# A gated cross-attention and mixture-of-experts block: Wout summed on VectorE, the last rounds reordered on each engine, the first list and rows fetched ahead of the stage barrier

## What is computed

```
x = x + tanh(g_xattn) * xattn(layernorm(x), ctx, ctx, mask)     # ctx: 8 x 722 x 512
x = x + tanh(g_ffn)   * moe(layernorm(x))

xattn: q = query@Wq+bq; k = key@Wk+bk; v = key@Wv+bv            # 32 wide
       s = q k^T / sqrt(512); s = (s - mean(s)) / (std(s) + eps)
       head = softmax(s + mask_term) @ v
       return tile(head, 16) @ Wout + bout                      # Wout: 512 x 512
moe:   p = softmax(x@router_w.T); w, idx = top_k(p, 2); w = w / (sum(w) + 1e-6)
       y = (silu(x@w13[:, :I]) * (x@w13[:, I:])) @ w2            # I = 1024, per expert
       return sum of w * y over the token's 2 experts
```

## Time and profile before

| | us |
|---|---|
| median of 3 runs | 453.95 |
| lowest and highest | 451.54, 454.06 |
| profiled execution, its own time | 455.68 |
| span of the profiled execution | 454.1 |
| stage one up to the barrier, in that span | 130.3 |
| start of the first product of tile 0 | 143.0 |
| start of the last tile's products | 425.0 |

### The profile page before, as it was taken

One profiled execution on the slowest core, in us unless ns is written; L12 is line 12 of the kernel. 1 busy time (PEld: TensorE's weight loads), 2 busy tenths in 40 slices (PEclk: granted clock), 3 DMA queues, 4 the chain that ended last, 5 costly groups with the idle time before them and its releaser, 6 DMA issues.

```text
span 454.1 us, 7292 instructions
## 1 busy us (share of the span) xinstructions
PE 391.5 (86%) x2056; PEld 288.7 (64%) x2057; DVE 232.1 (51%) x512; ACT 193.9 (43%) x314; POOL 123.0 (27%) x214
## 2 busy tenths in 40 slices
PE   2979989995105999999989999999999999999990
PEld 2425655553003878778767787787877878778780
DVE  2215665756681239528795223852962674565120
ACT  1123543432750247428765224643842662573220
POOL 2311354443412130412232123041122204314301
PEclk9989986976555999999999999999999999999997
DMA  8955779811106919727797221971774577201011
GB/s 260 370 192 180 270 230 367 313 50 37 36 0 206 396 25 282 274 64 214 255 387 296 84 46 27 279 289 33 228 258 145 129 287 225 46 0 29 19 27 15
DMA packets 17554, 78.01 MB, mean 172 GB/s; under 512 B 3618, under 2 KB 4770, under 8 KB 10372
## 3 DMA queue, kind: packets, MB, share of 16 engines
q1 hardware_dynamic: 11060, 66.79, 41.2%
q0 software_dynamic: 4720, 7.78, 8.9%
q10 hardware_dynamic: 1760, 3.28, 2.2%
HBM read 71.20 MB, written 7.54 MB: 173 GB/s over the span
## 4 chain that ended last, share of the span: by engine, by line
PE 75%; DVE 9%; issue 5%; ACT 3%; POOL 2%; DMA 2%; DVEq 1%; ACTq 1%; POOLq 0%
PE turnA L438 20%; PE scp L458 20%; PE turnB L438 18%; PE kvp L307 4%; PE kvp L445 3%; PE turnA L325 2%; PE scp L425 2%; DVE w13l L785 2%; PE scp L331 1%; PE turnA L363 1%; DMA xg<-xn_d,gidx 1%; DVE x L749 1%; ACT kv L504 1%; DVE bns L698 1%; PE turnA L356 1%
## 5 line engine op out<-in xcount | busy, mean ns | idle before, releaser
L785 DVE TENSOR_TENSOR w13l<-stage,w13h 128x1024 fp32r<-128x1024 f32 x64 | 76.4, 1219 | 3.8 <-ACT w13h L561 3.3
L561 ACT ACTIVATE w13h<-stage 128x1024 fp32r<-128x1024 f32 x64 | 64.5, 1052 | 0.1
L438 PE MATMUL turnA<-w13h,xTh 128*128 128x512 f32 x128 | 53.2, 415 | 5.0 <-DVE xTl L868 5.0
L458 PE MATMUL scp<-w2h,hTh 128*128 128x512 f32 x128 | 55.7, 435 | 1.2 <-DVE hTl L879 1.2
L438 PE MATMUL turnB<-w13h,xTh 128*128 128x512 f32 x128 | 51.9, 405 | 0.0
L438 PE MATMUL turnA<-w13h,xTl 128*128 128x512 f32 x128 | 51.3, 401 | 0.0
L438 PE MATMUL turnA<-w13l,xTh 128*128 128x512 f32 x128 | 51.3, 401 | 0.0
L458 PE MATMUL scp<-w2l,hTh 128*128 128x512 f32 x128 | 50.6, 395 | 0.0
L438 PE MATMUL turnB<-w13h,xTl 128*128 128x512 f32 x128 | 50.5, 395 | 0.0
L438 PE MATMUL turnB<-w13l,xTh 128*128 128x512 f32 x128 | 50.5, 394 | 0.0
L458 PE MATMUL scp<-w2h,hTl 128*128 128x512 f32 x128 | 50.2, 392 | 0.0
(11 more groups left out here) (162 smaller groups left out, 649.6 us busy)
## 6 DMA issues: line engine op xcount, KB each, us to landing
stage<-in_w_dram SPq DMA_DIRECT2D x48, 1024.0 KB, 6.9
ctx_t<-in_ctx_dram SPq DMA_DIRECT2D x8, 1444.0 KB, 9.0
x_t<-in_x_dram SPq DMA_DIRECT2D x8, 200.0 KB
xT_t<-in_xT_dram SPq DMA_DIRECT2D x8, 200.0 KB, 10.6
out_dram<-x ACTq DMA_DIRECT2D x8, 200.0 KB
xn_d<-xn ACTq DMA_DIRECT2D x8, 200.0 KB
stage<-in_wout_dram SPq DMA_DIRECT2D x1, 1024.0 KB, 11.8
ent_next<-lists_d POOLq DMA_DIRECT2D x17, 1.0 KB, 2.0
```

Source lines behind the costliest of these rows:

```text
L438: mm = pe.matmul(region, xp[:, c, :], wp[:, q, c, :], start=(c == 0 and i == 0), stop=(c == HC - 1 and i == 2))
L458: mm = pe.matmul(scp[:, 512:512 + H], hp[:, q, j * P:(j + 1) * P], wp[:, q * QC + j, :], start=(q == 0 and j == 0 and i == 0), stop=(q == ...
L561: act.activation(dst, src, ACT.Copy).then_inc(S["w_hi"], 1)
L785: dve.tensor_tensor(lo, raw, hi.bitcast(F32), ALU.subtract).then_inc(S["w_lo"], 1)
```

## The change

1. The sum of `Wout`'s four row blocks of 128 moves to VectorE: three adds of 128x512 (`add_wout`) between `make_values(0)` and `ln1_stats(2)`. TensorE then needs one product with `sel` per strip, where it had four, and adds `bout` with a product of one row, `ident[0:1, 0:D]`, so that `bout` is loaded once, to one row. `wraw` and its zeroing are gone; ScalarE scales with `g_t` while it copies to `wsum`, and VectorE's step between is gone. `sum_weights` stands ahead of `turn_query(1)`.
2. The transposes of `wsum` and the products with the router weights move to round 1: `turn_weights` behind `project(1)`, `route_weights` behind `scores(1)`, with the wait for `wx9` ahead of `heads(0)`. The transposes go to `outp`, so `turn_values(1)` waits for `wsumT_copied`. VectorE's copy to `wx9` stands behind `score_stats(1)`.
3. SyncE loads `bout`, then batch 1's context, then `Wout`, where it had `Wout`, `bout` twice, then the context.
4. TensorE's wait for `zero_made` moves from ahead of all rounds to `turn_values(0)`; `headT` is no longer zeroed.
5. VectorE: `finish_sigma(i)` stands ahead of `make_weights(i-2)` and `raw_logits(i-1)` in every round. After round 8 it runs `choose(7)`, `make_weights(6)`, `add_attention(7)`, `make_places(7)`, the tile tables, `make_weights(7)`, then its count on `attn_done`, and only then the splits of expert 0's units 0 to 7.
6. ScalarE: in round 8 `copy_head(7)` follows `copy_probT(7)`, ahead of the transfer and the normalisation of batch 6. Its splits 0 to 7 stand behind its count on `attn_done`.
7. GpSimd: `scatter` no longer waits for the scatter before it; in round 9 `scatter(6)` stands ahead of `norm2(7)`. The list entries and rows of tile 0 are fetched (`fetch_first`) before its count on `attn_done`; `xg`, `ent_next` and `gidx` get SBUF of their own for it.
8. `heads(b)` waits for `lg_made`, `outputs(b)` for `x2_ready` of the batch before.

```diff
@@ SyncE
+            sp.dma_start(bout_r[:], bout.rearrange("(o d) -> o d", o=1)).then_inc(S["bout_in"], 16)
+            load_ctx(1)
             sp.dma_start(stage2[:, 0:HC, :], Wout.rearrange("(c p) n -> p c n", p=P)).then_inc(S["wout_in"], 16)
-            sp.wait_ge(S["wraw_zero"], 1)
-            for r in range(2):
-                sp.dma_start(wraw[VW * r + D:VW * r + D + 1, :], bout.rearrange("(o d) -> o d", o=1)).then_inc(S["bout_in"], 16)
-            load_ctx(1)
@@ TensorE
             def turn_values(b):
                 pe.wait_ge(S["kv_copied"], b + 1)
+                if b == 0:
+                    pe.wait_ge(S["zero_made"], 1)
+                if b == 1:
+                    pe.wait_ge(S["wsumT_copied"], 1)
@@ heads, outputs
+                if b >= 1:
+                    pe.wait_ge(S["lg_made"], b)
...
+                if b >= 1:
+                    pe.wait_ge(S["x2_ready"], b)
...
             def sum_weights():
-                pe.wait_ge(S["wout_in"], 16)
+                pe.wait_ge(S["wout_added"], 3)
+                pe.wait_ge(S["bout_in"], 16)
                 pe.wait_ge(S["v_made"], 1)
-                for c in range(HC):
-                    for r in range(2):
-                        mm = pe.matmul(outp[r * VW:r * VW + D, :], sel[:], stage2[:, c, :], start=(c == 0), stop=(c == HC - 1))
+                for r in range(2):
+                    pe.matmul(outp[r * VW:r * VW + D, :], sel[:], stage2[:, HC, :], start=True, stop=True)
+                    mm = pe.matmul(outp[r * VW + D:(r + 1) * VW, :], ident[0:1, 0:D], bout_r[:], start=True, stop=True)
                 mm.then_inc(S["wsum_done"], 1)
+
+            def turn_weights():
...
+            def route_weights():
                 pe.wait_ge(S["wsumT_copied"], 1)
-                pe.wait_ge(S["q_fixed"], 4)
+                pe.wait_ge(S["q_fixed"], 6)
@@ TensorE, rounds
                 if live(i):
                     project(i)
+                if i == 1:
+                    turn_weights()
...
                     scores(i)
+                if i == 0:
+                    sum_weights()
+                if i == 1:
+                    route_weights()
+                    pe.wait_ge(S["wx9_made"], 1)
                 if live(i - 1):
                     heads(i - 1)
                 if live(i + 1):
                     turn_query(i + 1)
-                if i == 0:
-                    sum_weights()
@@ ScalarE, rounds
+                if i == NB:
+                    copy_head(i - 1)
                 if live(i - 2):
+                    if i >= NB:
+                        store_x2(i - 2)
                     normalise2(i - 2)
                     logit_exp(i - 2)
-                if live(i - 1):
+                if live(i - 1) and i < NB:
                     copy_head(i - 1)
...
-                if i == NB + 1:
-                    for unit in range(0, 2 * NQ):
-                        split_hi(0, unit, None)
             act.drain().then_inc(S["attn_done"], 1)
+            for unit in range(0, 2 * NQ):
+                split_hi(0, unit, None)
@@ VectorE, rounds
+                if i == NB + 1:
+                    break
...
                 if live(i - 2):
                     make_places(i - 2)
+                if live(i):
+                    finish_sigma(i)
+                if live(i - 2) and i < NB:
                     make_weights(i - 2)
                 if live(i - 1):
                     raw_logits(i - 1)
-                if live(i):
-                    finish_sigma(i)
-                if i == NB + 1:
-                    for unit in range(0, 2):
-                        split_lo(0, unit)
+            choose(NB - 1)
+            make_weights(NB - 2)
+            add_attention(NB - 1)
+            make_places(NB - 1)
...
-            for unit in range(2, 2 * NQ):
+            make_weights(NB - 1)
+            dve.drain().then_inc(S["attn_done"], 1)
+            for unit in range(0, 2 * NQ):
                 split_lo(0, unit)
-            dve.drain().then_inc(S["attn_done"], 1)
@@ GpSimd
                 for k in range(2):
-                    if b >= 1:
-                        pool.wait_ge(S[f"lists_put{k}"], 16 * b)
...
-                if live(i - 2):
+                if live(i - 2) and i <= NB:
                     norm2(i - 2)
                 if live(i - 3):
                     scatter(i - 3)
+                if i == NB + 1:
+                    norm2(i - 2)
...
+            def fetch_first():
+                pool.dma_start(ent_next[:], lists_d[0:P, :]).then_inc(S["list_in"], 16)
+                for k in range(2):
+                    pool.wait_ge(S[f"xn2_put{k}"], 16 * NB // 2)
+                gather(0)
...
+            fetch_first()
+            for k in range(2):
+                pool.wait_ge(S[f"out_put{k}"], 16 * NB // 2)
+            pool.drain().then_inc(S["attn_done"], 1)
+            pool.wait_ge(S["attn_done"], 4)
             pool.wait_ge(S["tiles_ready"], 1)
-            fetch(0)
             entries_stay(0)
```

More of the change, by code:

```diff
@@ L87, in gated_block @@
         tile_row = sb(es, "tile_row", [1, TILES], I32)
+        xg = sb(es, "xg", [P, H])
+        ent_next = sb(es, "ent_next", [P, 2], I32)
+        gidx = sb(es, "gidx", [P, 1], I32)
         a = ExitStack()
@@ L110, in gated_block @@
         wqr = sb(a, "wqr", [P, HC, VW + E])
-        wraw = sb(a, "wraw", [P, H])
+        bout_r = sb(a, "bout_r", [1, H])
         wsum = sb(a, "wsum", [P, H])
@@ L383, in _ @@
             pe.wait_ge(S["sel_made"], 1)
-            pe.wait_ge(S["zero_made"], 1)
             pe.wait_ge(S["wqr_made"], 3)
@@ L539, in copy_qT, with scale_weights, copy_turned_weights, store_x2 @@
                 act.activation(qT[b % 2][:], qTp, ACT.Copy, scale=float(H) ** -0.5).then_inc(S["qT_copied"], 1)
-            def wsum_steps():
+            def scale_weights():
                 act.wait_ge(S["wsum_done"], 1)
-                act.wait_ge(S["wraw_zero"], 1)
-                for r in range(2):
-                    act.activation(wraw[r * VW:r * VW + D, :], outp[r * VW:r * VW + D, :], ACT.Copy).then_inc(S["wraw_set"], 1)
+                act.wait_ge(S["tanh_done"], 1)
+                act.activation(wsum[:], outp, ACT.Copy, scale=g_t[:, 0:1]).then_inc(S["wsum_made"], 1)
+            def copy_turned_weights():
                 act.wait_ge(S["wsum_turned"], 1)
-                act.activation(wsumT[:].rearrange("p c s -> p (c s)"), turnB[:, 0:HC * P], ACT.Copy).then_inc(S["wsumT_copied"], 1)
+                act.activation(wsumT[:].rearrange("p c s -> p (c s)"), outp, ACT.Copy).then_inc(S["wsumT_copied"], 1)
+            def store_x2(b):
+                act.wait_ge(S["x2_ready"], b + 1)
+                act.dma_start(out[b], x2[b % 2][:]).then_inc(S[f"out_put{b % 2}"], 16)
             def split_hi(e, unit, last):
@@ L685, in make_values @@
                     dve.wait_ge(S["emask_made"], 1)
-                    dve.wait_ge(S["zero_made"], 1)
                 if b >= 2:
@@ L785, in split_lo, with add_wout, copy_low_weights @@
                 dve.tensor_tensor(lo, raw, hi.bitcast(F32), ALU.subtract).then_inc(S["w_lo"], 1)
-            def wsum_steps():
-                dve.wait_ge(S["wraw_set"], 2)
-                dve.wait_ge(S["bout_in"], 32)
-                dve.wait_ge(S["tanh_done"], 1)
-                dve.tensor_scalar(wsum[:], wraw[:], g_t[:, 0:1], None, ALU.mult).then_inc(S["wsum_made"], 1)
+            def add_wout():
+                dve.wait_ge(S["wout_in"], 16)
+                for j in range(2):
+                    dve.tensor_tensor(stage2[:, HC + j, :], stage2[:, 2 * j, :], stage2[:, 2 * j + 1, :], ALU.add).then_inc(S["wout_added"], 1)
+                dve.wait_ge(S["wout_added"], 2)
+                dve.tensor_tensor(stage2[:, HC, :], stage2[:, HC, :], stage2[:, HC + 1, :], ALU.add).then_inc(S["wout_added"], 1)
+            def copy_low_weights():
                 dve.wait_ge(S["wrw_done"], 1)
@@ L813, in _ @@
                     make_values(i)
+                if i == 0:
+                    add_wout()
                 if live(i + 2):
@@ L983, in _ @@
                 link(pool.memset(vn[j][:, :, D:VW], 0.0))
-            pool.memset(headT[:], 0.0).then_inc(S["zero_made"], 1)
+            pool.sem_inc(S["zero_made"], 1)
             pool.wait_ge(S["mask_in"], 16)
@@ L1037, in fetch, with gather @@
                 pool.dma_start(ent_next[:], lists_d[bass.ds(row, P), :]).then_inc(S["list_in"], 16)
+                gather(t)
+            def fetch_first():
[3 more added lines that the diff above has]
+                gather(0)
+            def gather(t):
                 hold(S["list_in"], 16 * t + 16)
```

28 lines of the change are left out of this document (10 added, 18 removed).

## The result

The changed kernel takes 460.52 us in the median of four runs (459.46 to 462.14), the kernel before on the same chip 453.94: a ratio of 1.015, 95% interval 1.011 to 1.020. It is slower by 6.6 us, where I forecast 6.4 us less; 460.5 lies outside my range, on the other side. In the experiments one of the ten runs of e5_sigma_back took 781.2 us, for a reason that no profile shows, and is left out of its ratio.

The account below looks back on a forecast made before the run. TensorE bounds stage two's tiles; in stage one no engine is full, so timelines and the chain that ended last decide. -3.5 + 1.8 - 4.7 = -6.4 us against the median of 453.95 gave 447.5, range 444 to 452.8.

Parts of the forecast that it names:

- Part 1, weight sum: Weight sum ahead of batch 1 and round 1: project(2) starts 3.5 us earlier (bounds -5 and -1.5).
- I take 1.9: Weight sum: the products after the three adds take 1.9 us, between 1.3 and 2.6.
- Part 2, `finish_sigma`: Round loop: finish_sigma ahead of make_weights and raw_logits costs 1.8 us over the rounds (bounds 0 and 5.5).
- 1.12 - 0.54: Round loop: price of about 0.6 us in a round where GpSimd starts the root of the score variance at once.
- the 11 that I named: Round 3 in the profile after: x2 comes 11 us after the x2 before.
- The rival of the loop: Round loop: each of rounds 3 to 7 pays 1.1 us, +5.5 in all, time 451.3; chance 0.20.
- Part 3, last rounds: Last rounds: scatter(6) ahead of norm2(7) makes batch 7's normalisation 1.2 us later; last scatter lands at 124.3.
- rival of the late lists: Fetch ahead of the barrier: slow gidx and later scatters cost 3 us at the barrier, time 450.5; chance 0.12.
- Part 4, fetch: Fetch ahead of the barrier: first product of tile 0 at 138.2 instead of 142.99, -4.7 us (bounds -6 and -2).
- GpSimd counts at 130.6: Fetch ahead of the barrier: with a gather issue of 2.2 us, GpSimd counts on the barrier at 130.6.
- next late are the down weights' splits: Road to tile 0: the down splits, not the gathered rows, come last, 6.6 us behind the barrier, at 137.2.
- Slower, by the clock: Rounds: the longer loop keeps TensorE at 1.2 GHz, 3.3 us per low round, +6.8 in all, 460.7; chance 0.05.

Follow-up runs that it names:

- e5_sigma_back: The changed kernel with finish_sigma(i) back behind make_weights(i-2) and raw_logits(i-1); ratio 1.005 to the kernel before.
- e8: e7 with GpSimd counting on the barrier by a bare increment instead of a drain; ratio 0.990 to the kernel before.
- e2: The kernel before with only tile 0's list and rows fetched ahead of GpSimd's drain; ratio 0.999 to the kernel before.
- e9: The kernel before with tile 0's list and rows fetched behind GpSimd's drain and count, ahead of its barrier wait; ratio 0.991 to the kernel before.
- e1: The kernel before with only items 1 to 4 and 8 of the change; ratio 1.008 to the kernel before.
- e3: The changed kernel with GpSimd's drain and count put ahead of the fetch of tile 0; ratio 1.008 to the kernel before.
- e7: The changed kernel with weight-sum products paired by form, finish_sigma behind the logits, norm2(7) ahead of scatter(6), drain and count ahead of the fetch; 448.95 us, ratio 0.988.
- e11: e7 with VectorE's first split waiting for a count behind the last scatter in GpSimd's program; ratio 0.988 to the kernel before.
- e12: e7 once more, nothing changed; 448.64 us, ratio 0.988 to the kernel before.
- e4: The changed kernel with the weight sum's four products in the order sel, sel, bout, bout; ratio 1.007 to the kernel before.

## Why the prediction was wrong, step by step

**Part 1, weight sum: -3.5 forecast, +2.8 measured.** The road to the products held: `Wout` landed at 19.9 (20.2), the adds were done at 21.9 (22.9), and from the products' end to `project(1)` it was 1.0 (1.0). The step that failed is "I take 1.9": 7.1. I had named the case that the `bout` products don't run beside the others and priced it at 2.6, and that is near what they take in pairs: 2.3 to 3.8 in the six kernels that have them so, by the clock. I missed that in the written order, `sel`, `bout`, `sel`, `bout`, nothing runs beside anything: each of the four takes what a pair takes, 1.92 us at the 1.2 GHz level (after, e8). And all but the first 0.3 us of them ran at that level. "TensorEngine Tiling (Array Packing)" of the Trainium skill has the rule, section "Key Properties": changing the tiling mode, not just the tile, drains TensorE. The traces agree, 7.1 us with three changes of form and 3.8 with one (e8), both at the 1.2 GHz level. That the mode is the reason isn't shown apart from this.

In round 1, `heads(0)` followed the projection's end by 6.1 us, as forecast (6.15). Mis-sized were the products: `project(1)` took 5.04, where I took 3.5, and from `heads(0)` to `project(2)` it was 2.95 for the 2.30 of before, with L362 at 1.73. `project(1)` ran at the 1.2 GHz level to its end, and the granted clock of the window 10 to 45 us fell from 0.90 to 0.77. So +1.9 became +3.9. Even with the products in pairs the front gains nothing: the six such kernels need 27.4 us on average from `project(0)` to `project(2)` (26.5 to 28.6), the three with the old front 27.5 (25.8 to 28.5). The clock has its part in that: over this stretch it was 0.78 to 0.84 in the six and 0.88, 0.93 and 0.88 in the three. Why the new front is granted less isn't shown. My base flattered the change as well: L363 took 5.15 in the trace of before, but 3.63 in e2 and e9, the same instructions at a granted clock of 1.00 for 0.70.

**Part 2, `finish_sigma`: mechanism right, size wrong.** +1.8 forecast, 2.8 in the trace of after, 4.0 over all profiles. The term that fell short is the price by round: I put 0 in round 2, 0.2 in 4 and 0.5 for two more, on the ground that the projection or the low clock hides it. From `x2` of batch 1 to that of batch 6, five loops, e1 needs 52.5 and e3 55.8, 0.65 per loop: which is nearly the 1.12 - 0.54 that I had worked out for a round in which GpSimd starts the root at once: on the average of these five nothing is hidden. The loop shown went from 9.92 to 11.21 us, the 11 that I named. The rival of the loop (+5.5) was too dear by 1.5, my term too cheap by 2.2.

**Part 3, last rounds: the reordering right, batch 7's scatters mis-priced.** 1.2 forecast for `scatter(6)` ahead of `norm2(7)`, 1.6 measured. The step that fell short is what follows: I priced batch 7's scatters at 0.99 although I had VectorE's splits begin at 120.4, above them. They took 1.61 and 1.87, and the list was loaded 3.0 us later than forecast, counted from batch 7's aggregation (25.5 for 22.5). Of these 3.0, 1.5 are the longer issues, 0.9 lie ahead of them (batch 7's weights were ready that much later), and the rest are gaps between the steps. My rival of the late lists also had 3 at the barrier, but that it is the same number is luck: it took 1.4 from the scatters and the rest from `gidx`, which took 0.76 here.

**Part 4, fetch: -4.7 forecast, +0.3 measured for the stretch, -3.0 with the drain moved (e3) and -4.6 with `norm2(7)` first as well (e7).** From list load to gather it was 3.95 (3.82); from barrier to first product 7.44 (7.6). "GpSimd counts at 130.6" failed: behind the gather stands a drain, which I had read in the quoted lines of the barrier and given no price. Gather and drain took 4.32 us, where I had 2.2 for the gather alone. The miss of this stretch, 41.2 for the forecast's 36.1, is thus 3.0 from the late list and 2.1 from the drain. e7, where the gather lies behind the count, has the forecast's length (36.2 for 40.9) by another road: its rows come last, not its down splits. My sentence "next late are the down weights' splits" was right for the change; that they hang on the barrier and the barrier on a landing was the part missed.

The rule of "SBUF — State Buffer" in the Trainium skill, section "SBUF: two separate sides", that a VectorE operation with two SBUF inputs and a GpSimd operation that reads SBUF exclude each other, is borne out: in all profiles the last scatters that begin while a split runs end 0.86 to 0.97 us behind its end, however long they waited, and those of the last two batches that begin with none running take 0.98 to 1.10. I had weighed the rule on the fetch and not on the scatters. The page names the descriptors of GpSimd's DMAs as locked out under another condition, a 2-port mode of VectorE, which no row here shows; whether a scatter is held by its descriptors or by the indices that it reads from SBUF stays open. e8 and e11 show that the waiting moves and doesn't go away: eight splits have to lie somewhere, and each place so far was ahead of a step of GpSimd's.

**The rivals.** "Slower, by the clock" (0.05) had the sign and, at 460.7, the number, but that is luck: it had the loss in four low-clock rounds of 3.3 each, 13.2 in all, and the rounds took 2.8 longer, at a granted clock of 0.82 for 0.86. Where the clock did cost was the front, 0.76 for 0.88 from `project(0)` to `project(2)`, and there it came on top of products that ran one by one. e7, with the same work in another order, is faster than before. I had no case in which several of the change's steps each cost what they were meant to save, and none for an operation that I had not priced.

**What stays open.** Whether the new front, its products in pairs, is worth anything against the old one: e7, e12 and e9 lie within 0.3%, less than their intervals. And how far the points at which the granted clock falls, which no edit here controls, decide what a stretch takes.

## What to carry to other kernels

Before moving work ahead of a barrier, list what the barrier's own instruction waits for: a drain behind an asynchronous transfer makes the barrier wait for its landing, and counting first and fetching behind the count gave here the 3.4 us back. Price each reordering on an engine by what the longest loop passes through, in every round, and take "hidden" only with a row that hides it. Where small products share the array, sort them by form: here it was worth 3.3 us at the same clock level.

## What the runs showed of the hardware

- GpSimd's drain took 1.369 us with nothing in flight (eight profiles, before, e7 and e9 among them), and 4.33 to 4.48 us behind an indirect DMA into SBUF (five), until its rows had landed.
- An increment that stands behind a DMA issue in GpSimd's program is made by its sequencer without waiting for that issue: in e11 at 117.29, the second scatter began at 118.30.
- Two 512-column float32 products into different 32-column strips run together when both have 128 rows (1.05 us for the pair in e4, as much as the first product alone in e3, both at the 2.4 GHz level; 1.92 at 1.2 GHz in e8) or both have one (1.92 at 1.2 GHz in e8), and one after the other when a product of 128 rows and one of a single row alternate (1.91 and 1.92 each at 1.2 GHz in the change).
- An indirect scatter's issue on GpSimd takes 0.98 to 1.10 us at the end of stage one when it begins with no split of VectorE's running; when one runs it waits for that one to end and ends 0.86 to 0.97 us behind it (up to 1.97 us in all). A gather's issue takes 1.08 alone and ends 0.95 us behind the split that it met (e7, e8, e11).
